# A decoder layer and a linear attention on one core: head rows spread by DMA, one-head blocks written by GpSimd

## The chip, the cores and the metric

The kernel runs on one core of a Trainium2 chip. The metric is the device time of one execution in microseconds. Engines are named as in the profile: PE is TensorE (PEld its weight loads), DVE is VectorE, ACT is ScalarE, POOL is GpSimd, SP is SyncE, which issues most DMAs.

## What is computed

The reference, cut to what matters (names as in the kernel; ln is a layer norm with gain and bias):

```python
def _mha(q_in, k_in, v_in, ..., mask):            # 16 heads of width 8, model width 128
    q = (q_in @ qw + qb).reshape(b, sq, 16, 8).transpose(0, 2, 1, 3)
    k, v = ...                                     # the same from k_in and v_in
    scores = einsum('bhqd,bhkd->bhqk', q, k) / sqrt(8)
    if mask is not None:
        scores = where(mask == 0, -1e9, scores)
    out = einsum('bhqk,bhkd->bhqd', softmax(scores), v)
    return out.transpose(0, 2, 1, 3).reshape(b, sq, 128) @ ow + ob

x = x + mha(x, x, x, mask);        x = ln(x, g1, be1)     # x: 16 x 128 x 128 f32
x = x + mha(x, ctx, ctx, None);    x = ln(x, g2, be2)     # ctx: 16 x 77 x 128
x = x + relu(x @ w1 + b1) @ w2 + b2;  x = ln(x, g3, be3)
# linear attention of x over ctx
KV = elu(ctx).T @ ctx;  Z = 1 / (elu(x) . sum(elu(ctx)) + 1e-6)
out = ln(x + (elu(x) @ KV) * Z, gamma, beta)
```

## The kernel before

The batch of 16 is taken in 8 groups of two items (G = 2). A group goes through a pipeline of iterations: iteration i projects q, k and v of self-attention (kind "s") for group i + 1 (stage NEXT = -1), runs the two self-attention jobs of group i (SELF), the two cross-attention jobs (kind "c") of group i - 1 (CROSS), the feed-forward part and the linear attention of group i - 2 (TAIL) and the output of group i - 3 (LAST). Each iteration has four steps k = 0 to 3, called steps below. In step k one job is "current": s of item 0, s of item 1, c of item 0, c of item 1. For the current job PE forms the scores a second time with keys on the partitions (`key_major`, L344), ACT takes the exponential (L564) and PE multiplies with V (`times_v`, L360). For the job after it PE forms the scores with queries on the partitions (`query_major`, L321) only for the row maxima, which DVE takes (L714). For the job before it PE transposes and projects (L380, L385, L389), DVE adds the residual and takes the moments (L752 to L763), POOL forms the inverse root (`inverse_root`, L942), DVE standardises (L770), and POOL writes the residual of the next stage (`next_residual`, L949, L951). So step 0 prepares maxima for s of item 1, step 1 for c of item 0, step 2 for c of item 1, and step 3 for s of item 0 of the next group.

Each engine has its own queue of instructions, written in the order of the same loops (`iteration` in each engine's block), and stands at the first semaphore wait that is not met. `PROJ_USES` (L86) lists at which step and which quarter u of it a projection or a transpose uses one of two PSUM banks.

A score product contracts over 128 partitions although a head has only 8 columns. Four heads, the "unit" u, are handled together, and q and k are first split into a high and a low bf16 part (`split_hi` on ACT, L597; `split_lo` on DVE, L780). Then the "head rows" are built: for a unit, 32 rows of the four heads are repeated four times over the partitions, as hi/lo of q against hi/lo of k. PE does this by eight products with 0/1 matrices for a kind, side and item (`spread_rows`, L457, products at L465 and L467; the uses sq0, sk0, cq0, ck0 and so on), and ACT copies the result out (`copy_rows`, L600, L611). From the rows of q DVE makes four one-head blocks (`widen`, L785, copies at L790): the rows times a column that is 1 on the partitions of head j and 0 elsewhere (`row_is_j`). `query_major` waits for these blocks (`wide_s`, `wide_c`) of its item and for the rows of k before its first product.

Iterations 3 to 6 are a loop on the device (`run_iterations`, L120), the others are written out.

## Time and profile before

| | us |
|---|---|
| runs (3) | 342.73, 343.69, 345.12; median 343.69 |
| the profiled execution | 342.77 |
| its span in the profile | 340.70 |
| one iteration in the middle | 36.3 |

The profile is of the one execution of 342.77 us; 2.07 us of it lie around the span. The page gives each engine's busy time, and a view of windows gives it for single stretches with the clock granted to TensorE (1.00 is full). The timeline gives instructions in order of time with start and duration; merged ones have a count (x4), and in brackets how long the engine had been idle before and what ended that.

### The profile page before, as it was taken

The numbers are of one execution on the slowest core, as the hardware profiler recorded it, in microseconds if no ns is written. First come the engines' busy times: TensorE is split into PE (matmuls) and PEld (weight loads), VectorE is DVE, ScalarE is ACT, GpSimd is POOL, SyncE is SP. The second block draws the span as 40 slices with busy tenths as digits, with TensorE's granted clock in tenths as the row PEclk, the third lists the DMA queues.
The fourth block names the chain that finished last, engine by engine and source line by source line (L and its number), as shares of the span: only waits on it lengthen the run. The fifth ranks groups of instructions, "written<-read, shape, count | busy, mean of one in ns | idle before, by whom it ended". The sixth has DMA issues, their size and how long they took to land.

```text
span 340.7 us, 8979 instructions
## 1 busy us (share of the span) xinstructions
PE 289.0 (85%) x3056; PEld 197.5 (58%) x3056; DVE 261.5 (77%) x867; ACT 174.5 (51%) x386; POOL 76.0 (22%) x136
## 2 busy tenths in 40 slices
PE   3769789989999999989998999899988986788551
PEld 2534555766775667656665676567755754565331
DVE  7664787878698979898898979897989784765524
ACT  2215445756565566646664656465754655336220
POOL 0410200211132112212231214112222224202421
PEclk9979999999999999999999999999999999589695
DMA  7500000000000000100000000000000000000000
GB/s 223 187 0 3 17 9 3 27 3 9 2 27 3 12 0 17 29 9 0 15 25 9 0 15 25 0 9 0 25 1 11 2 26 2 0 15 11 2 15 15
DMA packets 7506, 6.85 MB, mean 20 GB/s; under 512 B 744, under 2 KB 6712, under 8 KB 7480
## 3 DMA queue, kind: packets, MB, share of 16 engines
q1 hardware_dynamic: 7048, 6.38, 6.3%
q8 instruction: 15, 0.25, 0.3%
q10 hardware_dynamic: 432, 0.14, 0.2%
q14 instruction: 11, 0.09, 0.1%
HBM read 5.46 MB, written 1.05 MB: 19 GB/s over the span
## 4 chain that ended last, share of the span: by engine, by line
PE 54%; DVE 24%; issue 10%; ACT 5%; POOL 3%; DVEq 1%; DMA 1%; ACTq 0%; POOLq 0%; SPq 0%
PE proj_ps L399 10%; PE av_ps L370 7%; DVE neg_max L714 5%; PE s_ps L357 5%; PE s_ps L353 5%; PE s_ps L335 4%; PE proj_ps L465 3%; PE s_ps L332 3%; PE proj_ps L405 3%; POOL rstd L942 3%; PE s_ps L351 3%; PE proj_ps L467 2%; PE post_ps L389 2%; PE proj_ps L424 2%; PE post_ps L385 2%
## 5 line engine op out<-in xcount | busy, mean ns | idle before, releaser
L564 ACT ACTIVATE probs<-s_ps 128x512 f32<-128x512 f32 (+1 forms) x128 | 76.2, 595 | 57.4 <-PE s_ps L357 56.1
L714 DVE TENSOR_REDUCE neg_max<-s_ps 128x4 f32<-128x512 f32 (+1 forms) x128 | 71.6, 576 | 9.5 <-PE s_ps L335 9.2
L942 POOL TENSOR_TENSOR rstd<-var_e,neg_half 128x1 f32<-128x1 f32 x32 | 17.5, 547 | 181.8 <-DVE var_e L763 181.8
L357 PE MATMUL s_ps<-max_x,unit_sel 128*128 128x512 bf16 (+1 forms) x128 | 49.0, 383 | 3.6 <-DVE max_x L728 3.4
L399 PE MATMUL proj_ps<-x_t,w_sb 128*128 128x256 f32 x80 | 26.6, 455 | 1.0 <-issue 0.6
L335 PEld LDWEIGHTS s_ps<-sk_rows,sq_wide 128*128 128x128 bf16 x256 | 20.6, 101 | 10.3 <-issue 1.6
L570 ACT COPY av_sb<-av_ps 128x256 f32<-128x256 f32 x32 | 11.9, 372 | 27.3 <-PE av_ps L370 27.3
L335 PE MATMUL s_ps<-sk_rows,sq_wide 128*128 128x128 bf16 x256 | 25.7, 225 | 0.0
L332 PE MATMUL s_ps<-bias_q,id_b 128*128 128x512 bf16 x64 | 25.4, 397 | 0.0
L353 PE MATMUL s_ps<-cq_wide,ck_rows 128*77 128x512 bf16 x64 | 24.8, 387 | 0.0
L351 PE MATMUL s_ps<-bias_k,id_b 128*128 128x512 bf16 x64 | 24.7, 386 | 0.0
L353 PE MATMUL s_ps<-sq_wide,sk_rows 128*128 128x512 bf16 x64 | 24.5, 383 | 0.0
L728 DVE TENSOR_TENSOR max_x<-s_ps,max_is_j 128x512 bf16<-128x512 bf16 x32 | 22.1, 691 | 2.2 <-PE s_ps L342 2.1
L790 DVE TENSOR_SCALAR sq_wide<-sq_rows,row_is_j 128x512 bf16<-128x512 bf16 x64 | 20.3, 380 | 2.9 <-ACT sq_rows L611 2.9
L370 PE MATMUL av_ps<-probs,v_aug_s 128*32 128x128 f32 x512 | 20.6, 279 | 1.7 <-ACT probs L564 1.7
L357 PEld LDWEIGHTS s_ps<-max_x,unit_sel 128*128 128x128 bf16 (+1 forms) x128 | 13.8, 108 | 14.1 <-DVE max_x L728 7.3
L370 PE MATMUL av_ps<-probs,v_aug_c 77*32 77x128 f32 x512 | 20.6, 279 | 1.4 <-ACT probs L564 1.2
L335 PEld LDWEIGHTS s_ps<-ck_rows,cq_wide 128*128 128x128 bf16 x256 | 17.2, 101 | 6.5 <-DVE neg_max L714 0.3
L619 ACT ACTIVATE hid<-proj_ps,col_sb 128x256 f32<-128x256 f32 x32 | 13.4, 471 | 14.7 <-PE proj_ps L399 14.7
L335 PE MATMUL s_ps<-ck_rows,cq_wide 128*128 128x77 bf16 x256 | 19.9, 203 | 0.2 <-DVE neg_max L714 0.2
L752 DVE TENSOR_TENSOR x_post<-post_ps,r 128x128 f32<-128x128 f32 x32 | 9.2, 288 | 13.4 <-PE post_ps L389 13.3
L399 PEld LDWEIGHTS proj_ps<-x_t,w_sb 128*128 128x128 f32 x80 | 15.4, 217 | 6.0 <-issue 3.4
(131 smaller groups left out, 657.7 us busy)
## 6 DMA issues: line engine op xcount, KB each, us to landing
xt_in<-in_x_t SPq DMA_DIRECT2D x8, 128.0 KB, 2.0
out<-o_all SPq DMA_DIRECT2D x8, 128.0 KB, 1.8
row_sb<-in_rows SPq DMA_DIRECT2D x1, 832.0 KB, 6.5
w_sb<-in_weights SPq DMA_DIRECT2D x1, 768.0 KB, 10.4
ct_in<-in_ctx_t SPq DMA_DIRECT2D x8, 77.0 KB, 1.8
cn_in<-in_ctx_n SPq DMA_DIRECT2D x8, 77.0 KB
w_sb<-in_weights SPq DMA_DIRECT2D x2, 128.0 KB, 2.8
id_f<-in_ident ACTq DMA_DIRECT2D x1, 64.0 KB, 2.6
```

What stands on the lines that cost most here:

```text
L332: nc.tensor.matmul(bank[:, :], id_b[:], bias_q[:].unsqueeze(1).to_broadcast([P, RH, n]), start=True, stop=False, skip_group_check=True)
L335: last = nc.tensor.matmul(bank[:, j * n:(j + 1) * n], wide[kind][:, b, j, u, :], rows_qk[kind + "k"][:, b, u, :], start=(kind == "c"), sto ...
L351: nc.tensor.matmul(bank[:, :], id_b[:], bias_k[:].unsqueeze(1).to_broadcast([P, RH, S]), start=True, stop=False)
L353: nc.tensor.matmul(bank[0:n, :], rows_qk[kind + "k"][:, b, u, :], wide[kind][:, b, :, u, :], start=(kind == "c"), stop=False)
L357: nc.tensor.matmul(bank[0:n, :], unit_sel[:, u, 0:n], max_x[:, b, :, :], start=False, stop=True).then_inc(M["s2_ready"], 1)
L370: last = nc.tensor.matmul(av_ps[32 * r:32 * r + VW, rr * S:(rr + 1) * S], v_aug[kind][:, b, u, r, :], probs[0:KLEN[kind], u, r * S:(r + 1) ...
L399: return nc.tensor.matmul(bank[:, at:at + n], w_sb[:, w, :], src, start=True, stop=True)
L564: nc.scalar.activation(probs[0:n, u, :], s2_ps[u % 2][0:n, :], ACT.Exp, scale=SCALE).then_inc(M["exp_done"], 1)
L714: nc.vector.tensor_reduce(neg_max[:, b, RH * u:RH * (u + 1)], scores, AX_X, ALU.max, negate=True).then_inc(M["max_done"], 1)
L728: nc.vector.tensor_tensor(max_x[:, b, :, :], nmt_ps.unsqueeze(1).to_broadcast([P, RH, S]), max_is_j[:].unsqueeze(2).to_broadcast([P, RH, S ...
L790: last = nc.vector.tensor_scalar(wide[name[0]][:, b, j, :, :], rows_qk[key][:, b, :, :], row_is_j[:, j:j + 1], None, ALU.mult)
L942: nc.gpsimd.tensor_tensor(rstd[:, b, :], var_e[:, b, :], neg_half[:, 0:1], ALU.pow).then_inc(M["rstd_ready"], 1)
```

## The change

Three things change together. First, the head rows are no longer spread by PE. The columns of the q and k weights and biases are permuted on the host, so that the row of head j, column c, unit u lies at partition (j, c, u) with u innermost, and four DMAs from SBUF to SBUF for each side write the rows: repeat s goes to partitions s, s + 4, s + 8 and so on. That is eight DMAs for each kind and group, all issued by SP. The products with 0/1 matrices, their two PSUM uses and ACT's copies go. Second, the one-head blocks are written by POOL, for both items of a group at once: four instructions of 1024 elements (4 units x 2 items x 128) for each kind and group. Kind c is written in step 0, after `next_residual` of that step; kind s in steps 1 and 2, two heads each, after `next_residual`. Third, what that needs: blocks and k rows have two buffers (group parity), so have `xt_in` and `ct_in`, which are loaded an iteration earlier, and all twelve iterations are written out, with no loop.

```diff
-        ("yc0", TAIL, 0, 0), ("cv", CROSS, 0, 0), ("cq0", CROSS, 0, 1), ("ck0", CROSS, 0, 2), ("sqk", NEXT, 0, 3),
...
+        ("yc0", TAIL, 0, 0), ("cv", CROSS, 0, 0), ("sqk", NEXT, 0, 3),
...
-    def run_iterations(eng, iteration):
-
-        for i in range(NEXT, TAIL + 1):
-            iteration(i)
-        with eng.Fori(TAIL + 1, NG - 1) as i:
-            iteration(i)
-        for i in range(NG - 1, NG + LAST):
+    def run_iterations(iteration):
+
+        for i in range(NEXT, NG + LAST):
             iteration(i)
...
-                rows_qk[key] = sb(f"{key}_rows", [P, G, UNITS, n], BF16)
-            wide[kind] = sb(f"{kind}q_wide", [P, G, RH, UNITS, S], BF16)
+            rows_k[kind] = sb(f"{kind}k_rows", [P, 2, UNITS, G, KLEN[kind]], BF16)
+            rows_q[kind] = sb(f"{kind}q_rows", [P, UNITS, G, S], BF16)
+            wide[kind] = sb(f"{kind}q_wide", [P, 2, RH, UNITS, G, S], BF16)
...
+        def wait_spread(eng, key, g):
+
+            eng.wait_ge(M["spread_" + key], 16 * 4 * (g + 1))
...
+            def spread_rows(i, name):
+
+                kind = name[0]
+                g = i - (NEXT if kind == "s" else SELF)
+                wait_read(sp, i, name)
+                wait_reuse(sp, M["wide_" + kind], RH * g)
+                for s in range(4):
+                    sp.dma_start(rows_q[kind][s:P:4, :, :, :].rearrange("p u b n -> p u (b n)"),
+                                 part_of(kind + "q", s)[:].rearrange("p b n -> p (b n)")).then_inc(
+                        M[f"spread_{kind}q"], 16)
+                s2_done(sp, kind, g - 2)
+                for s in range(4):
+                    sp.dma_start(rows_k[kind][s:P:4, g % 2, :, :, :].rearrange("p u b n -> p u (b n)"),
+                                 part_of(kind + "k", s)[:].rearrange("p b n -> p (b n)")).then_inc(
+                        M[f"spread_{kind}k"], 16)
...
                 if u == 0:
-                    pe.wait_ge(M[f"wide_{kind}"], G * g + b + 1)
-                    wait_rows(pe, kind, "k", b, g)
+                    pe.wait_ge(M["wide_" + kind], RH * (g + 1))
+                    wait_spread(pe, kind + "k", g)
...
-                for u in range(UNITS):
-                    nc.tensor.matmul(bank[:, u * n:(u + 1) * n], spread[side, "hi"][:, u, :, :],
-                                     hi[kind + side][:, b, :], start=True, stop=False)
...
-                nc.scalar.copy(rows_qk[name[:2]][:, b, :, :], proj_ps[bank_of(name)][:, 0:UNITS * n].rearrange(
-                    "p (u n) -> p u n", u=UNITS)).then_inc(read(name), 1)
...
-                for j in range(RH):
-                    last = nc.vector.tensor_scalar(wide[name[0]][:, b, j, :, :], rows_qk[key][:, b, :, :],
-                                                   row_is_j[:, j:j + 1], None, ALU.mult)
...
+            def widen(kind, g, heads):
+
+                wait_spread(pool, kind + "q", g)
+                s2_done(pool, kind, g - 2)
+                for j in heads:
+                    nc.gpsimd.tensor_scalar(wide[kind][:, g % 2, j, :, :, :], rows_q[kind][:], row_is_j[:, j:j + 1],
+                                            None, ALU.mult).then_inc(M["wide_" + kind], 1)
...
                     if prev:
                         inverse_root(*prev)
                         next_residual(*prev)
+                    if k == 0 and on(i, CROSS):
+                        widen("c", i - CROSS, range(RH))
+                    if k in (1, 2) and on(i, NEXT):
+                        widen("s", i - NEXT, range(2 * k - 2, 2 * k))
...
+    rows_first = np.arange(d).reshape(UNITS, RH, hd).transpose(1, 2, 0).reshape(d)
+    for n in ("sa_qw", "sa_kw", "ca_qw", "ca_kw", "sa_qb", "sa_kb", "ca_qb", "ca_kb"):
+        a[n] = a[n][..., rows_first]
```

How the order moves, first on POOL, from step 0 to step 2 of an iteration in which all stages run. Before (rstd, y_g and r are the inverse root, the product with the gain and the residual; rstd_l and rstd_f belong to the last two norms):

```order
L942 TENSOR_TENSOR rstd<-var_e,neg_half 128x1
L949 TENSOR_TENSOR y_g<-y_n,row_sb 128x128
L951 TENSOR_TENSOR r<-y_g,res_bias 128x128
L960 TENSOR_TENSOR rstd_l<-var_l,neg_half 128x2
L942 TENSOR_TENSOR rstd<-var_e,neg_half 128x1
L949 TENSOR_TENSOR y_g<-y_n,row_sb 128x128
L951 TENSOR_TENSOR r<-y_g,res_bias 128x128
L964 TENSOR_TENSOR rstd_f<-var_f,neg_half 128x2
L942 TENSOR_TENSOR rstd<-var_e,neg_half 128x1
```

And now, at the same place:

```order
L934 TENSOR_TENSOR r<-y_g,res_bias 128x128
L920 TENSOR_SCALAR cq_wide<-cq_rows,row_is_j 128x1024 x4
L945 TENSOR_TENSOR rstd_l<-var_l,neg_half 128x2
L925 TENSOR_TENSOR rstd<-var_e,neg_half 128x1
L932 TENSOR_TENSOR y_g<-y_n,row_sb 128x128
L934 TENSOR_TENSOR r<-y_g,res_bias 128x128
L920 TENSOR_SCALAR sq_wide<-sq_rows,row_is_j 128x1024 x2
L949 TENSOR_TENSOR rstd_f<-var_f,neg_half 128x2
L925 TENSOR_TENSOR rstd<-var_e,neg_half 128x1
L932 TENSOR_TENSOR y_g<-y_n,row_sb 128x128
L934 TENSOR_TENSOR r<-y_g,res_bias 128x128
L920 TENSOR_SCALAR sq_wide<-sq_rows,row_is_j 128x1024 x2
```

The four copies of kind c stand behind the residual of step 0, the four of kind s behind those of steps 1 and 2.

On PE, the end of step 0 and the first products of step 1, with their waits. Before (nm_parts are the maxima being transposed, the two products with xt_in are the projection sqk, and L335 is the first product of `query_major` for kind c):

```order
L342 MATMUL s_ps<-id_b,nm_parts 128x128 [waits nm_ready]
L485 ISA
L118 REGISTER_ALU [waits xt_loaded]
L399 MATMUL proj_ps<-xt_in,w_sb 128x256 [waits proj_read0]
L399 MATMUL proj_ps<-xt_in,w_sb 128x256
L325 ISA
L252 REGISTER_ALU [waits wide_c]
L118 ISA [waits proj_read1]
L335 MATMUL s_ps<-ck_rows,cq_wide 128x77 [waits max_done]
```

And now:

```order
L365 MATMUL s_ps<-id_b,nm_parts 128x128 [waits nm_ready]
L422 MATMUL proj_ps<-xt_in,w_sb 128x256 [waits proj_read0,xt_loaded0]
L422 MATMUL proj_ps<-xt_in,w_sb 128x256
L358 MATMUL s_ps<-ck_rows,cq_wide 128x77 [waits max_done,spread_ck,wide_c]
L358 MATMUL s_ps<-ck_rows,cq_wide 128x77 x3
L393 MATMUL av_ps<-probs,v_aug_s 32x128 [waits exp_done]
```

The place of the first product of step 1 on PE is the same; its wait now asks for the blocks of both items, written by POOL, and for the k rows from the DMAs.

## Rows read from the trace of the kernel before

**Rows 1.** Page, part 1: engine busy us (share of the span) xinstructions.

```profile
PE 289.0 (85%) x3056; PEld 197.5 (58%) x3056; DVE 261.5 (77%) x867; ACT 174.5 (51%) x386; POOL 76.0 (22%) x136
```

**Rows 2.** Windows: length, busy PE, PEld, DVE, ACT, POOL (xcount), granted clock.

```profile
21.00:24.20 3.20, 3.20 (x15) 1.71 (x14) 1.68 (x3) 0.60 (x1) 0.00 (x0) 0.50 0.00 0
163.34:199.67 36.33, 34.37 (x384) 23.73 (x383) 31.43 (x106) 21.45 (x48) 8.69 (x17) 1.00 0.04 12
```

**Rows 3.** Groups by line and shape, VectorE: the copies into one-head blocks.

```profile
L790 DVE TENSOR_SCALAR sq_wide<-sq_rows,row_is_j 128x512 bf16<-128x512 bf16 x64 | 20.3, 380 | 2.9 <-ACT sq_rows L611 2.9
L790 DVE TENSOR_SCALAR cq_wide<-cq_rows,row_is_j 128x512 bf16<-128x512 bf16 x64 | 18.2, 347 | 0.4 <-ACT cq_rows L611 0.3
```

**Rows 4.** Timeline (start us, us, engine, line), steady iteration, spread by TensorE.

```profile
173.99 0.22 PE L465 MATMUL proj_ps<-sq_hi,spread_q_hi 128*128 128x128 bf16 x1
174.44 0.39 PE L380 MATMUL post_ps<-id_f,av_sb 128*128 128x128 f32 x2
...
187.94 0.21 PE L465 MATMUL proj_ps<-ck_hi,spread_k_hi 128*128 128x77 bf16 x1
188.23 0.46 PE L389 MATMUL post_ps<-w_sb,att_t 128*128 128x128 f32 x2
```

**Rows 5.** Timeline, steady iteration, step 0 into step 1.

```profile
190.15 0.55 POOL L942 TENSOR_TENSOR rstd<-var_e,neg_half 128x1 f32<-128x1 f32 x1 [6.25 <-DVE var_e L763]
190.15 0.30 PE L335 MATMUL s_ps<-ck_rows,cq_wide 128*128 128x77 bf16 x4
...
191.83 0.45 POOL L951 TENSOR_TENSOR r<-y_g,res_bias 128x128 f32 x1 [0.22 <-POOL y_g L949]
```

**Rows 6.** Timeline, same iteration, step 2 into step 3.

```profile
171.87 0.38 PE L332 MATMUL s_ps<-bias_q,id_b 128*128 128x512 bf16 x1
...
172.25 0.55 POOL L942 TENSOR_TENSOR rstd<-var_e,neg_half 128x1 f32<-128x1 f32 x1 [3.52 <-DVE var_e L763]
...
173.91 0.45 POOL L951 TENSOR_TENSOR r<-y_g,res_bias 128x128 f32 x1 [0.19 <-POOL y_g L949]
```

**Rows 7.** Groups by line and shape, GpSimd, and the tile sq_rows (min/median/max ns).

```profile
L949 POOL TENSOR_TENSOR y_g<-y_n,row_sb 128x128 f32<-128x128 f32 x32 | 14.8, 461 | 14.8 <-DVE y_n L770 14.8
...
L934 POOL TENSOR_TENSOR r<-x_all,row_sb 128x2048 f32<-128x2048 f32 x1 | 4.5, 4507 | 11.9 <-DMA x_all<-in_x 11.9
...
L790 DVE TENSOR_SCALAR sq_wide<-sq_rows,row_is_j x64: 341/346/2100, 9.6 to 250.0; 128x512 bf16<-128x512 bf16 x64
```

**Rows 8.** Timeline, start of the program.

```profile
11.57 0.63 PE L332 MATMUL s_ps<-bias_q,id_b 128*128 128x512 bf16 x1
...
15.33 3.28 DVE L790 TENSOR_SCALAR sq_wide<-sq_rows,row_is_j 128x512 bf16<-128x512 bf16 x4
...
17.71 0.49 POOL L936 TENSOR_TENSOR res_bias<-row_sb 128x128 f32<-128x128 f32 x1
...
19.69 0.23 PE L342 MATMUL s_ps<-id_b,nm_parts 128*128 128x128 bf16 x1 [4.12 <-DVE nm_parts L721]
...
20.34 0.38 PE L351 MATMUL s_ps<-bias_k,id_b 128*128 128x512 bf16 x1
```

**Rows 9.** Timeline, iteration 0 and iteration 8.

```profile
39.98 0.46 POOL L951 TENSOR_TENSOR r<-y_g,res_bias 128x128 f32<-128x128 f32 x1
...
43.95 0.10 PEld L342 LDWEIGHTS s_ps<-id_b,nm_parts 128*128 128x128 bf16 x1 [1.45 <-DVE nm_parts L721]
...
292.36 0.68 PE L335 MATMUL s_ps<-ck_rows,cq_wide 128*128 128x77 bf16 x8
...
295.13 0.45 POOL L951 TENSOR_TENSOR r<-y_g,res_bias 128x128 f32<-128x128 f32 x1
```

**Rows 10.** Page, part 6 (KB each, us to landing), and timeline: DMA issue and low parts.

```profile
xt_in<-in_x_t SPq DMA_DIRECT2D x8, 128.0 KB, 2.0
...
12.23 0.43 SPq L304 DMA_DIRECT2D ct_in<-in_ctx_t  x1
...
180.34 0.37 DVE L780 SCALAR_TENSOR_TENSOR ck_lo<-proj_ps,col_sb,ck_hi 128x154 bf16<-128x154 f32 x1
```

More of the change, by code:

```diff
@@ L86, in decoder_layer_kernel @@
     PROJ_USES = [
-        ("yc0", TAIL, 0, 0), ("cv", CROSS, 0, 0), ("cq0", CROSS, 0, 1), ("ck0", CROSS, 0, 2), ("sqk", NEXT, 0, 3),
-        ("yc1", TAIL, 1, 0), ("cq1", CROSS, 1, 0), ("ck1", CROSS, 1, 1), ("h01", TAIL, 1, 1), ("h23", TAIL, 1, 2),
-        ("ff", TAIL, 1, 4),
-        ("ys0", SELF, 2, 0), ("sq0", NEXT, 2, 0), ("sk0", NEXT, 2, 1), ("kv", TAIL, 2, 2), ("sv", NEXT, 2, 3),
-        ("yt", TAIL, 2, 4),
-        ("ys1", SELF, 3, 0), ("sq1", NEXT, 3, 0), ("sk1", NEXT, 3, 1), ("cqk", SELF, 3, 2), ("la", TAIL, 3, 3)]
+        ("yc0", TAIL, 0, 0), ("cv", CROSS, 0, 0), ("sqk", NEXT, 0, 3),
+        ("yc1", TAIL, 1, 0), ("h01", TAIL, 1, 1), ("h23", TAIL, 1, 2), ("ff", TAIL, 1, 4),
+        ("ys0", SELF, 2, 0), ("kv", TAIL, 2, 2), ("sv", NEXT, 2, 3), ("yt", TAIL, 2, 4),
+        ("ys1", SELF, 3, 0), ("cqk", SELF, 3, 2), ("la", TAIL, 3, 3)]
     USE_NAMES = [name for name, *_ in PROJ_USES]
@@ L144, in decoder_layer_kernel @@
         id_b = sb("id_b", [P, P], BF16)
-        spread = {(side, part): sb(f"spread_{side}_{part}", [P, UNITS, 4, 32], BF16)
-                  for side in "qk" for part in ("hi", "lo")}
         row_is_j = sb("row_is_j", [P, RH])
@@ L541, in iteration @@
                     light_work(i, k, UNITS)
-            run_iterations(pe, iteration)
+            run_iterations(iteration)
         @block.scalar
@@ L676, in _ @@
                 nc.vector.memset(v_aug[kind][:], 0.0)
-            for tile in spread.values():
-                nc.vector.memset(tile[:], 0.0)
             nc.vector.memset(cn_in[:, :, D:D + 1], 1.0).then_inc(M["zeros_set"], 1)
```

115 lines of the change are left out of this document (48 added, 67 removed).

## The prediction

> **What bounds the kernel now.** I read the page's busy shares first, then the windows of single iterations, then the timeline of one steady iteration line by line, and last the start and the end. The page shows TensorE (PE) at 85% and VectorE (DVE) at 77%, ScalarE (ACT) at 51%, and GpSimd (POOL) at 22% [rows 1]. In a steady iteration, from 163.34 to 199.67, it is clearer: of 36.33 us PE is busy 34.37 and DVE 31.43, at the full clock, and POOL only 8.69 [rows 2]. So PE's queue sets the pace: 1.96 us of it are idle. By that view it looks right to take work from PE and DVE and give some to POOL. The timeline must say whether POOL gives it back in time, since PE takes its instructions in order and stands at the first wait that is not met.
>
> **What is removed.** PE's spread of head rows goes: eight matmuls of 128 columns take from 173.99 to 174.44, 0.45 us, and eight of 77 columns from 187.94 to 188.23, 0.29 us [rows 4]. A steady iteration has six of the first kind (sq0, sq1, sk0, sk1, cq0, cq1) and two of the second (ck0, ck1): 6 x 0.45 + 2 x 0.29 = 3.3 us of PE. ACT's eight copies out of PSUM behind them go, and DVE's sixteen copies into one-head blocks, 20.3 + 18.2 us in all [rows 3], which is 4.8 us for each of 8 groups. PE's 1.96 us of idle time come mostly from waits on such ACT and DVE work; I take 1.5 us of them as gained. Together 4.8 us for each of the iterations 2 to 6, that is 24 us. Iterations 0, 1, 7 and 8 hold only parts of this work; I put them at 8 us together (1, 2.5, 2.5, 2). Gain: 32 us.
>
> **What is added on the DMA queue.** Sixteen DMAs for a group. A neighbouring row shows 0.43 us to issue one, and 2.0 us for 128 KB to land [rows 10]; each new one moves 64 KB (or 39) in 128 pieces. Four q DMAs are thus in place about 4 x 0.43 + 2.0 = 3.7 us after the low part is written, all eight after 5.4. For kind c the low part ends at 180.71 [rows 10] and POOL first turns to the rows at 192.28 [rows 5]: 11.6 us of cover. For kind s the cover is about step 0's end to step 1's end, nearly as much. The DMAs cost nothing unless each takes some 3 us by itself. The second buffer of xt_in and ct_in, and the unrolled loop, I put at nothing: PE hardly waits for loads, and iterations written out in the program before (2, and 7 on) look like the loop's.
>
> **What is added on POOL, and where.** Each group and kind now has four POOL instructions of 1024 elements. No row shows this operation on POOL. With two f32 inputs it takes 461 ns for 128 elements and 4507 ns for 2048 [rows 7], so (4507 - 461) / 1920 = 2.11 ns an element and 191 ns fixed; 1024 elements would be 2.35 us, the upper end. The lower end is DVE's own pace for it: 18.2 us for 64 copies of 512 elements [rows 3], 0.284 us each, so 0.57 us for 1024. The new instruction reads one stream, not two; half the slope gives 0.191 + 1024 x 1.055 ns = 1.27 us. I take T = 1.27, as the row of the same engine is nearer than DVE's.
>
> What matters is the place in the queue. At step 0 POOL does rstd, y_g and the residual r for the job before, and then the four copies of kind c, with no wait between. DVE's and POOL's part of that chain begins with PE's L389 of the same step and can't come earlier: L389 starts at 188.23 [rows 4], rstd at 190.15, y_g follows, r ends at 191.83 + 0.45 = 192.28 [rows 5]. But PE comes to the first product that needs the c blocks (L335, the first of step 1) at 190.15 [rows 5]. The blocks are there at 192.28 + 4T. PE therefore stands still for 2.13 + 4T = 7.2 us. In the kernel before, DVE writes these blocks during step 0, and only those of one batch item.
>
> At step 2 the same happens with kind s. Half of its copies come at step 1, where they are harmless (rstd_f comes about when they end). The other two come after r of step 2, which ends at 173.91 + 0.45 = 174.36, while PE is at step 3's first product (L332) at 171.87 [rows 6]: 2.49 + 2T = 5.0 us of waiting. Behind both waits stand PE's remaining key-major products and products with V, for which ACT and DVE wait in turn, so nothing makes these 12.2 us good; PE's work before and after is full.
>
> Ends without the pattern: **start.** POOL is held by r0 and the two bias sums until 17.71 + 0.49 = 18.20 [rows 8]; then come 4T, so the first product starts at 23.3 where it was 11.57. The way from there to the first L351 was 8.8 us; without DVE's 3.28 us of widening and PE's spread about 4.8. So L351 comes at 28.1 where it was 20.34: 7.8 us. **Iteration 0:** r ends at 40.44, blocks at 43.0, four products with their maxima then take about 4.4 us to L342, against 43.95 [rows 9]: 3.4 us. **Iteration 1:** c has no residual ahead, but its DMAs and 4T take about 9 us: 3 us; s as above, 5.0. **Iterations 2 to 6:** 5 x 12.2 = 61.2. **Iteration 7:** c, 7.2. **Iteration 8:** r ends at 295.58, PE is there at 292.36 [rows 9]: 3.2 + 4T = 8.3. Sum of waits: 95.9 us.
>
> **The clock.** At the start PE stood for 4.12 us before 19.69 [rows 8], and the stretch from 21.00 to 24.20 then ran at 0.50 of the clock, 1.2 GHz where it was 2.4 before, with PE busy all the time [rows 2]. Such a stretch costs 3.1 / 2 = 1.55 us. Twelve to fourteen of the new waits are longer than that one: 13 x 1.55 = 20 us.
>
> Sum, against the profiled execution's 342.77 us: - 32 + 95.9 + 20 = 427. The runs' median is 343.69; I forecast **427 us**, 24% slower.
>
> **Where the skill is weighed.** The rows put one POOL copy between 0.57 and 2.35 us. The Trainium skill, "GPSIMD Engine Reference", Performance versus the Vector engine, gives a port-bound 1.03 cycles an element for a short one-input body and 769 ns measured for 512 elements; by the first figure an estimate of T is 1.07 us and the sum 417, by the second twice 769 ns, 1.54 us, and 440. No run here shows either. In [rows 8] four DVE copies took 3.28 us instead of 4 x 0.284 = 1.14 beside a long POOL instruction, one of them 2100 ns [rows 7]; "SBUF — State Buffer" calls this pair of ports an exclusive lock, and the trace agrees. It can delay single DVE instructions by up to T here, at times when DVE has slack, so it changes neither sum nor chances.
>
> **Rivals.** The sum has 50 us for each us of T (4 at the start, 2 + 4 + 2 in iterations 0 and 1, 30 in 2 to 6, 4 + 4 at the end).
> (a) *POOL needs the two-input time*, T = 2.35: 427 + 54 = 481. For it: it is the engine's only measured slope. Against: half the data is read, in bf16.
> (b) *Shorter copies and no clock loss*: at T = 0.57 the waits are 4.4 and 3.6 us; 427 - 35 - 20 = 372. For it: such short waits are near or below the one that cost the clock. T = 1.27 with no clock loss gives 407.
> (c) *The DMAs are late*: if each of the q DMAs of kind c took 4 us one after another, 16 us against 11.6 of cover, 4.4 us more for 7 groups: 458. Against: issue and landing in [rows 10].
> (d) *Not slower: the blocks are ready when PE comes*, so that only the gain is left, 343 - 32 = 311 us. The place is PE's first product of steps 1 and 3. It decides where 2.13 + 4T and 2.49 + 2T fall to nothing; no T does that, since r alone ends after PE arrives. It needs PE to reach these products later than now for another reason, above all that it is held by DVE's maxima. Without clock loss the sum breaks even at T of about 0.1 us, less than any POOL row.
>
> **How the numbers follow.** Forecast (T from 0.9 to 1.6, with most of the clock loss: 405 to 445) 0.62; (a), T well above that, 0.13; (b), 372 to 405, 0.17; (c) 0.04; (d) 0.03, and 0.01 that the parts cancel. The range, 388 to 470, leaves out the outer half of (a) and of (b). About 1% is what a measurement can tell here: faster 0.03, same 0.01, slower 0.96.
>
> **What would show it.** Right: PE idle before L358 (the old L335 and, with its bias, L332) and put down to POOL's widening or its row copies, 7 and 5 us long, once each an iteration; POOL's four copies back to back at 1.27 us each right behind r; an iteration of some 47 us; a granted clock of 0.5 in parts; PE, DVE and ACT busy for smaller shares. Wrong: copies of POOL that end before PE arrives, waits on the DMAs in their place, iterations near 31 us.

## The result and the profile after

The changed kernel takes 533.64 us (median of 4 runs, 532.5 to 535.74) against 344.02 us of the kernel before on the same chip: ratio 1.552, 95% interval 1.544 to 1.560. The forecast was 427 us with a range of 388 to 470. The sign and the place were right, the size was not. The profiled execution took 532.5 us, with a span of 530.7.

The page of the kernel after, part 1 and the granted clock of part 2, against [rows 1]:

```profile
PE 295.0 (56%) x2522; PEld 190.6 (36%) x2544; DVE 233.4 (44%) x727; ACT 145.6 (27%) x322; POOL 257.0 (48%) x200
...
PEclk9998586878696959578687959578686958955876
```

PE has 534 matmuls fewer and is yet busy for longer, since part of them ran at half the clock (the run e6 below has the same 2522 recorded matmuls in 260.5 us). POOL's 76.0 us have become 257.0. No engine is busy for much more than half of the span, which says that they wait for each other in turn. The chain of the work that ended last says for whom:

```profile
POOL 37%; PE 36%; DVE 15%; issue 7%; DMA 2%; ACT 1%; SPq 1%; POOLq 0%; DVEq 0%
POOL cq_wide L920 17%; POOL sq_wide L920 13%; PE av_ps L393 6%; PE proj_ps L422 5%; PE s_ps L358 5%; PE s_ps L376 4%; PE s_ps L355 3%; POOL rstd L925 3%; PE s_ps L380 3%; PE s_ps L374 2%; DMA x_all<-in_x 2%; DVE y_n L757 2%; DVE st L745 2%; PE post_ps L412 2%; DVE x_post L739 2%
```

The groups of POOL's copies (L920; busy and mean of one, then idle time before) and PE's waits (total, times, longest):

```profile
L920 POOL TENSOR_SCALAR cq_wide<-cq_rows,row_is_j 128x1024 bf16<-128x1024 bf16 x32 | 90.5, 2849 | 10.9 <-DMA cq_rows<-cq_lo 10.9
L920 POOL TENSOR_SCALAR sq_wide<-sq_rows,row_is_j 128x1024 bf16<-128x1024 bf16 x32 | 90.9, 2853 | 0.1
```

```profile
PE s_ps L358 <- POOL cq_wide L920: 101.8, 8, 14.6
PE s_ps L355 <- POOL sq_wide L920: 78.9, 8, 22.9
```

One copy takes 2.85 us. I had taken 1.27 and set 2.35 as the upper end. PE waits for them 8 + 8 times, 180.7 us together, where I had summed 95.9 (at the start the 22.9 us are the whole wait, while my sum counts only the delay). In the timeline of a middle iteration the places are those of [rows 5] and [rows 6]: r, then the copies in one piece, then PE.

```profile
245.44 0.45 POOL L934 TENSOR_TENSOR r<-y_g,res_bias 128x128 f32<-128x128 f32 x1
245.87 11.31 POOL L920 TENSOR_SCALAR cq_wide<-cq_rows,row_is_j 128x1024 bf16<-128x1024 bf16 x4
257.24 0.44 PE L358 MATMUL s_ps<-ck_rows,cq_wide 128*128 128x77 bf16 x4 [12.93 <-POOL cq_wide L920]
...
279.08 0.45 POOL L934 TENSOR_TENSOR r<-y_g,res_bias 128x128 f32<-128x128 f32 x1
279.51 5.67 POOL L920 TENSOR_SCALAR sq_wide<-sq_rows,row_is_j 128x1024 bf16<-128x1024 bf16 x2
285.24 0.61 PE L355 MATMUL s_ps<-bias_q,id_b 128*128 128x512 bf16 x1 [6.55 <-POOL sq_wide L920]
```

That iteration (243.90 to 303.23) lasts 59.33 us where 36.33 were before [rows 2]. The windows show it whole, then the first wait, and the three stretches behind idle time at about half the clock (the last columns are granted clock, DMA share, GB/s):

```profile
243.90:303.23 59.33, 35.77 (x316) 23.20 (x319) 29.01 (x90) 17.92 (x41) 31.35 (x25) 0.80 0.09 24
...
247.00:257.20 10.20, 0.00 (x0) 0.00 (x0) 0.00 (x0) 0.00 (x0) 10.18 (x4) 0.55 0.18 51
```

```profile
257.20:262.00 4.80, 4.76 (x37) 2.81 (x38) 1.95 (x9) 1.73 (x4) 0.00 (x0) 0.53 0.00 0
...
275.50:278.70 3.20, 3.18 (x14) 2.24 (x12) 2.72 (x10) 0.97 (x2) 0.70 (x2) 0.50 0.02 5
285.20:289.30 4.10, 4.06 (x31) 2.39 (x32) 0.81 (x2) 0.97 (x2) 1.39 (x2) 0.53 0.00 0
```

From 247.0 to 257.2 not one instruction runs on PE, DVE or ACT. The half clock covers 12.1 us of the iteration, PE nearly always busy in them, so by an estimate it adds some 6 us.

### The profile page after: what moved, and what is told of

Read it like the earlier page. It is cut to its first block, busy times and chain, and to the rows that moved or that the text cites. A ratio compares the mean times of both kernels' runs of the same rounds, so it can differ in the third digit from the quotient of the medians.

```text
span 530.7 us, 7271 instructions
## 1 busy us (share of the span) xinstructions
PE 295.0 (56%) x2522; PEld 190.6 (36%) x2544; DVE 233.4 (44%) x727; ACT 145.6 (27%) x322; POOL 257.0 (48%) x200
## 3 DMA queue, kind: packets, MB, share of 16 engines
HBM read 5.46 MB, written 1.05 MB: 12 GB/s over the span
## 4 chain that ended last, share of the span: by engine, by line
POOL 37%; PE 36%; DVE 15%; issue 7%; DMA 2%; ACT 1%; SPq 1%; POOLq 0%; DVEq 0%
POOL cq_wide L920 17%; POOL sq_wide L920 13%; PE av_ps L393 6%; PE proj_ps L422 5%; PE s_ps L358 5%; PE s_ps L376 4%; PE s_ps L355 3%; POOL rstd L925 3%; PE s_ps L380 3%; PE s_ps L374 2%; DMA x_all<-in_x 2%; DVE y_n L757 2%; DVE st L745 2%; PE post_ps L412 2%; DVE x_post L739 2%
## 5 line engine op out<-in xcount | busy, mean ns | idle before, releaser
L920 POOL TENSOR_SCALAR cq_wide<-cq_rows,row_is_j 128x1024 bf16<-128x1024 bf16 x32 | 90.5, 2849 | 10.9 <-DMA cq_rows<-cq_lo 10.9
L920 POOL TENSOR_SCALAR sq_wide<-sq_rows,row_is_j 128x1024 bf16<-128x1024 bf16 x32 | 90.9, 2853 | 0.1
L358 PE MATMUL s_ps<-ck_rows,cq_wide 128*128 128x77 bf16 x256 | 22.9, 223 | 105.1 <-POOL cq_wide L920 101.8
L355 PE MATMUL s_ps<-bias_q,id_b 128*128 128x512 bf16 x64 | 30.2, 472 | 85.1 <-POOL sq_wide L920 78.9
L358 PEld LDWEIGHTS s_ps<-ck_rows,cq_wide 128*128 128x128 bf16 x256 | 19.1, 115 | 116.7 <-POOL cq_wide L920 104.8
L380 PE MATMUL s_ps<-max_x,unit_sel 128*77 128x512 bf16 (+1 forms) x106 | 45.0, 424 | 0.0
L355 PEld LDWEIGHTS s_ps<-bias_q,id_b 128*128 128x128 bf16 x64 | 7.2, 113 | 84.0 <-POOL sq_wide L920 58.2
L358 PE MATMUL s_ps<-sk_rows,sq_wide 128*128 128x128 bf16 x256 | 30.0, 250 | 0.0
L358 PEld LDWEIGHTS s_ps<-sk_rows,sq_wide 128*128 128x128 bf16 x256 | 24.1, 115 | 14.4 <-issue 8.6
L374 PE MATMUL s_ps<-bias_k,id_b 128*128 128x512 bf16 x64 | 26.9, 420 | 0.0
L393 PE MATMUL av_ps<-probs,v_aug_c 77*32 77x128 f32 x512 | 24.1, 314 | 1.4 <-ACT probs L570 1.2
L932 POOL TENSOR_TENSOR y_g<-y_n,row_sb 128x128 f32<-128x128 f32 x32 | 14.8, 463 | 15.0 <-DVE y_n L757 15.0
L945 POOL TENSOR_TENSOR rstd_l<-var_l,neg_half 128x2 f32<-128x2 f32 x8 | 6.4, 804 | 31.9 <-DVE var_l L801 31.9
```

The lines of the kernel that those rows point to most:

```text
L355: nc.tensor.matmul(bank[:, :], id_b[:], bias_q[:].unsqueeze(1).to_broadcast([P, RH, n]), start=True, stop=False, skip_group_check=True)
L358: last = nc.tensor.matmul(bank[:, j * n:(j + 1) * n], wide[kind][:, g % 2, j, u, b, :], rows_k[kind][:, g % 2, u, b, :], start=(kind == "c ...
L374: nc.tensor.matmul(bank[:, :], id_b[:], bias_k[:].unsqueeze(1).to_broadcast([P, RH, S]), start=True, stop=False)
L380: nc.tensor.matmul(bank[0:n, :], unit_sel[:, u, 0:n], max_x[:, b, :, :], start=False, stop=True).then_inc(M["s2_ready"], 1)
L393: last = nc.tensor.matmul(av_ps[32 * r:32 * r + VW, rr * S:(rr + 1) * S], v_aug[kind][:, b, u, r, :], probs[0:KLEN[kind], u, r * S:(r + 1) ...
L920: nc.gpsimd.tensor_scalar(wide[kind][:, g % 2, j, :, :, :], rows_q[kind][:], row_is_j[:, j:j + 1], None, ALU.mult).then_inc(M["wide_" + ki ...
```

## The experiments

Theory: the time is PE's waits for POOL's copies right behind r, so it follows their place and their price T. Rivals: the row DMAs or their issue; the clock; the written-out loop; VectorE held by POOL; and that the gain I had assumed is not there. "Middle iteration" is one of the iterations 2 to 6. The kernel before, measured beside these runs, had medians of 343.4 to 344.7 us. e2 to e5 and e11 were executed once each, the others four times or more. e2 and e6 leave out scores, so they are no kernels to be used, only measurements.

**e1, one part undone: VectorE widens.**

```diff
-                    if k == 0 and on(i, CROSS):                 # POOL
-                        widen("c", i - CROSS, range(RH))
-                    if k in (1, 2) and on(i, NEXT):
-                        widen("s", i - NEXT, range(2 * k - 2, 2 * k))
+                if k == 0 and u in (2, 3) and on(i, CROSS):     # VectorE
+                    widen("c", i - CROSS, range(2 * u - 4, 2 * u - 2))
+                if k == 2 and u < 4 and on(i, NEXT):
+                    widen("s", i - NEXT, [u])
```

> The changed kernel with one thing undone: the one-head blocks are written by VectorE again (four instructions of 1024 elements for a kind and group: kind c at quarters 2 and 3 of step 0, kind s one in each quarter of step 2). The DMAs, the double buffers and the written-out iterations stay. Theory (all of the loss is PE's wait for POOL's copies, and what the clock loses behind it; spreading by DMA is the gain I worked out): the waits for widening are under 1 us each, PE's 3.3 us of spreading an iteration are gone, and VectorE, busy 31.4 us of a 36.3-us iteration before, sets the pace: iterations of 32 to 34 us, total 322 us (312 to 335). Rival A (the sixteen DMAs of a group or SP's 0.6 us for each are part of the loss): PE or VectorE waits on the row DMAs, over 360 us. Rival B (the written-out loop costs): over 345 with no waits of this kind.

Measured: 359.46 us, ratio 1.045 (1.039 to 1.051). POOL's part is 174 of the 190 us, as the theory says. But nothing of a gain is to be seen behind it: without POOL's copies the kernel is still 15 us slower than before. The theory's 322 missed. Rival A does not hold either: a middle iteration has no wait on row DMAs. The time fits rival B's, but not its cause, as e14 shows. PE does 3.4 us less and the iteration takes 37.31 us:

```profile
200.03:237.34 37.31, 30.96 (x320) 20.29 (x318) 30.45 (x98) 17.82 (x40) 9.12 (x16) 1.00 0.13 36
```

PE waited 1.8 and 1.4 us for blocks that VectorE writes last in their step, and 1.7 us for `att`.

**e2, half of the dose.** Heads 1 and 3 of each unit are left out of the widening.

```diff
-                        widen("c", i - CROSS, range(RH))
+                        widen("c", i - CROSS, range(0, RH, 2))
...
-                        widen("s", i - NEXT, range(2 * k - 2, 2 * k))
+                        widen("s", i - NEXT, [2 * k - 2])
```

> The changed kernel with POOL writing the blocks of heads 0 and 2 of each unit only; the blocks of heads 1 and 3 stay zero, so half of the scores are left out of the widening, with PE's products unchanged. It halves the number of POOL copies at every place. Theory (the time follows 4T, 2T and the like, with T = 2.85 us measured, 50 T in the sum): half of 50 x 2.85 = 71 us less, 462 us (450 to 475); PE's wait at L358 7.2 us and at L355 3.7 us in a middle iteration, where they are 12.9 and 6.6. Rival (the waits are set by something else that POOL's widening only happens to follow, or another wait takes the place): 500 us or more.

Measured: 448.76 us, 85 us less, and waits in a middle iteration of 7.3 and 3.7 us. The waits came out as expected. The time is just below the expected 450 to 475: it fell by more than the 50 T of the sum.

**e3, PE kept busy in the waits.**

```diff
+                    if b == 0 and (kind == "c" or g > 0):
+                        for _ in range(46 if kind == "c" else 22):
+                            nc.tensor.matmul(s1_ps[0][:, :], id_b[:], bias_q[:].unsqueeze(1).to_broadcast([P, RH, S]),
+                                             start=True, stop=True, skip_group_check=True)
                     pe.wait_ge(M["wide_" + kind], RH * (g + 1))
```

> The changed kernel with PE doing idle products of 512 columns into the free score bank ahead of the two waits for the blocks, 46 of them (9.9 us at 0.216 us each) before L358 of kind c, 22 (4.75 us) before L355 of kind s. Waits end when POOL ends, as before, but PE is not idle in them. Theory (of the 534 us some 40 are products at half the clock behind the waits): in a middle iteration of the changed kernel the stretches 257.2 to 261.9 and 285.2 to 289.2 run at half clock, which is 2.3 + 2.0 us; gone, they give 4.3 us for each of 7 iterations, total 503 us (495 to 512). Rival (the half clock is beside the path, the pace is set by POOL and VectorE): 530 or more.

Measured: 524.62 us, 9 us less, and middle iterations of 58.0 to 58.2. The expectation of 503 missed. The filling ended 3 us before the blocks came, and the clock fell behind it all the same, only later and for less time (two windows of that run):

```profile
197.80:200.40 2.60, 2.56 (x31) 1.77 (x32) 0.94 (x3) 0.97 (x2) 0.00 (x0) 0.77 0.00 0
200.40:203.00 2.60, 2.60 (x12) 1.82 (x11) 1.86 (x10) 1.36 (x3) 0.72 (x1) 0.57 0.03 6
```

So this run took away only part of what it was to take away. It shows that the clock is a share of the loss, not its size. The size is read better from e6, which has the same 316 recorded products in a middle iteration: PE is busy for 30.36 us there, and for 35.77 in the iteration shown above, 5.4 us more.

**e4, the price of a copy by itself.**

```diff
+            then(nc.gpsimd.tensor_scalar(tb[1][:, 0:1024], tb[0][:, 0:1024], c0, None, ALU.mult))
+            then(nc.gpsimd.tensor_scalar(tb[1][:, 0:512], tb[0][:, 0:512], c0, None, ALU.mult))
...
```

> The changed kernel, and behind its last store eleven instructions on POOL alone, nothing else running, each behind the one before, to price the copy: with a column as the factor 1024, 512 and 2048 bf16 elements; with a constant as the factor, 1024 bf16; with a column, 1024 f32; a plain copy of 1024 bf16 and of 1024 f32; the product of two tensors of 1024, f32 and bf16. Theory (the price is POOL's own, by element, and neither VectorE nor the DMAs lengthen it): the 1024-element one takes 2.85 us as inside the kernel, 512 take 1.5, 2048 take 5.6; f32 in place of bf16 about the same or less; the f32 product of two tensors 2.35 us by the slope read before (rows of r0 and of y_g). Rival (it is long only in the kernel, by contention for SBUF): 1.3 us or less for 1024 alone.

The timeline of POOL, behind the last store, with nothing else running (0/1 column as the factor for 1024, 512 and 2048; a constant; f32; plain copies; products of two tensors):

```profile
535.67 2.85 POOL L979 TENSOR_SCALAR tb<-tb,row_is_j 128x1024 bf16<-128x1024 bf16 x1
538.62 1.56 POOL L980 TENSOR_SCALAR tb<-tb,row_is_j 128x512 bf16<-128x512 bf16 x1
540.28 5.44 POOL L981 TENSOR_SCALAR tb<-tb,row_is_j 128x2048 bf16<-128x2048 bf16 x1
545.80 2.77 POOL L982 TENSOR_SCALAR tb<-tb 128x1024 bf16<-128x1024 bf16 x1
548.67 2.84 POOL L983 TENSOR_SCALAR tf<-tf,row_is_j 128x1024 f32<-128x1024 f32 x1
551.58 1.04 POOL L984 COPY tb<-tb 128x1024 bf16<-128x1024 bf16 x1
552.67 1.04 POOL L985 COPY tf<-tf 128x1024 f32<-128x1024 f32 x1
553.80 2.34 POOL L986 TENSOR_TENSOR tf<-tf 128x1024 f32<-128x1024 f32 x1
556.22 2.12 POOL L987 TENSOR_TENSOR tb<-tb 128x1024 bf16<-128x1024 bf16 x1
```

Alone it takes the same 2.85 us: no contention. From 512 to 2048 elements it grows by 3.88 / 1536 = 2.53 ns an element, with 0.27 us fixed. The type makes no difference to it, a constant factor almost none. With one stream it is dearer than the product of two tensors (2.34), whose slope I had halved. A plain copy costs 1.04.

**e5, the lower price in the same places.** Since a head's rows lie on 32 partitions of their own, plain copies of these into blocks zeroed once give the same blocks.

```diff
-                    nc.gpsimd.tensor_scalar(wide[kind][:, g % 2, j, :, :, :], rows_q[kind][:], row_is_j[:, j:j + 1],
-                                            None, ALU.mult).then_inc(M["wide_" + kind], 1)
+                    nc.gpsimd.tensor_copy(wide[kind][32 * j:32 * j + 32, g % 2, j, :, :, :],
+                                          rows_q[kind][32 * j:32 * j + 32]).then_inc(M["wide_" + kind], 1)
...
```

> The changed kernel with POOL's product with a 0/1 column replaced by a plain copy of the 32 partitions of the head into blocks that are zeroed once at the start; same places, same number (four for kind c behind r in step 0, two and two for kind s in steps 1 and 2). A plain copy of 1024 bf16 elements took 1.04 us alone, so T goes from 2.85 to 1.04, below the 1.27 us that I had assumed. Theory (place right, T wrong): by the slope of the run with half of the heads, (533.6 - 448.8) / 1.43 = 59 us for each us of T, 533.6 - 1.81 x 59 = 426 us; by the prediction's own sum 427 - 0.23 x 50 = 415. So 410 to 432, with waits of 5.7 us at L358 and 3.0 us at L355 in a middle iteration. Rival (a fixed cost of the POOL path, not the price of its copies): over 460.

Measured: 435.43 us, just above the expected 410 to 432, with waits of 6.0 and 4.2 us in a middle iteration. From here to the changed kernel it is 98.2 us for 1.81 us of T, 54 for each; the prediction's sum had 50.

**e6, no widening at all** (the scores are left out; VectorE zeroes the blocks once at the start, and PE waits for the row DMAs).

```diff
-                    pe.wait_ge(M["wide_" + kind], RH * (g + 1))
+                    wait_spread(pe, kind + "q", g)
...
+            for kind in "sc":
+                nc.vector.memset(wide[kind][:], 0.0)
...
```

> The changed kernel with the widening left out altogether: the blocks stay zero, PE waits for the row DMAs of q and k alone. So all products, maxima and DMAs remain and the scores are left out. It shows what spreading by DMA can give at most, my 'gain of 32 us'. By the prediction 343.5 - 32 = 311 us, somewhat less still, as VectorE's 4.5 us of widening an iteration are gone too. Rival, after the run with VectorE's widening came at 359 with PE idle 6.4 us of a 37.3-us iteration: PE's freed time turns into waits for the round trips through VectorE and ScalarE and for the DMAs, so 325 to 340. Rival C: the start alone (rows by DMA are later than by PE) costs some 4 us of either.

Measured: 334.85 us, ratio 0.970 (0.966 to 0.975). So without any widening the gain is 9 us, not 32; the forecast's 311 missed, and the rival's 325 to 340 holds. A middle iteration, and PE's only long wait for blocks or rows, at the start:

```profile
153.32:187.12 33.80, 30.36 (x316) 20.37 (x319) 27.16 (x90) 17.71 (x41) 8.72 (x17) 1.00 0.15 42
```

```profile
PE s_ps L354 <- DMA sk_rows<-sk_lo: 18.0, 1, 18.0
```

But this start is not that of the changed kernel: e6's own zeroing delays it. Its timeline, and then the first row DMA of the changed kernel:

```profile
3.88 3.47 DVE L671 MEMSET sq_wide<- 128x4096 uint32 x1 [0.80 <-issue]
8.15 3.47 DVE L671 MEMSET cq_wide<- 128x4096 uint32 x1 [0.80 <-issue]
13.01 4.52 DVE L691 TENSOR_SCALAR bias_q<-mask_q_i 128x128 bf16<-128x128 int32 x1
17.45 0.47 DVE L768 SCALAR_TENSOR_TENSOR sq_lo<-proj_ps,col_sb,sq_hi 128x256 bf16<-128x256 f32 x1
18.34 1.27 SPq L277 DMA_DIRECT2D sq_rows<-sq_hi  x2
```

```profile
10.09 1.27 SPq L278 DMA_DIRECT2D sq_rows<-sq_hi  x2
```

The row DMAs start 8.25 us later than in the changed kernel. An estimate without this delay is 334.9 - 8.2 = some 327 us, a ceiling of 17 us for the gain; it was not run.

**e7, the two kinds divided** (plain copies; kind s on POOL, all four in step 1; kind c on VectorE at quarters 1 and 2 of step 0) and **e8, all on VectorE** (plain copies, kind s at quarters 0 and 1 of step 2).

```diff
+                if k == 0 and u in (1, 2) and on(i, CROSS):     # VectorE, both runs
+                    widen("c", i - CROSS, range(2 * u - 2, 2 * u))
+                    if k == 1 and on(i, NEXT):                  # POOL, e7
+                        widen("s", i - NEXT, range(RH))
+                if k == 2 and u in (0, 1) and on(i, NEXT):      # VectorE, e8
+                    widen("s", i - NEXT, range(2 * u, 2 * u + 2))
```

> The plain copies of 32 partitions, divided: kind s by POOL, all four behind r in step 1 (4 x 1.04 = 4.2 us, wanted only at step 3), kind c by VectorE at quarters 1 and 2 of step 0, earlier than in the run in which VectorE did all. Nothing of POOL's copies stands between r and a product that waits. Theory: PE's waits for blocks under 1 us each, iterations of 34 us instead of 37.3, total 335 us (325 to 345). Rival (VectorE and ScalarE round trips set the pace whatever the blocks do): 350 or more. It is also the candidate for a kernel that beats the one before.

> Both kinds by VectorE with the plain copies of 32 partitions, kind c at quarters 1 and 2 of step 0, kind s at quarters 0 and 1 of step 2, two at a time. Against the first run (VectorE, product with a column, 525 ns each, later places, 359.5 us) it changes place and price. If a plain copy takes about half, 0.27 us, VectorE has 2 us more in an iteration: 338 us (328 to 348). Rival (place and price don't matter, the round trips do): 352 to 360.

Measured: 355.81 us (ratio 1.034, 1.029 to 1.038) and 360.26 us (1.043, 1.037 to 1.049). Both missed. Earlier and cheaper copies bring a middle iteration at the full clock down to 35.4 us in e7 and 35.7 in e8, below the 36.33 before. But the start is 11 us later than before (the first rstd begins at 43.99 and 44.55, in the kernel before at 33.31), and not all middle iterations ran at the full clock: one of e7's five took 38.6 us and three of e8's 38.7, each at a granted clock of 0.91. e8's trace is of the slowest of its four executions, 363.12 us.

**e9, other places at the lower price.**

```diff
+                    if k == 0 and on(i, CROSS):
+                        widen("c", i - CROSS, range(RH))
                     if prev:
                         inverse_root(*prev)
                         next_residual(*prev)
-                    if k == 0 and on(i, CROSS):
-                        widen("c", i - CROSS, range(RH))
-                    if k in (1, 2) and on(i, NEXT):
-                        widen("s", i - NEXT, range(2 * k - 2, 2 * k))
+                    if k == 1 and on(i, NEXT):
+                        widen("s", i - NEXT, range(RH))
```

> The run with POOL's plain copies (435.4 us, T = 1.04) with only POOL's order changed: kind c's four copies stand ahead of the inverse root of step 0, in the time in which POOL waited for var_e, and kind s's four all behind r of step 1. Price and number of the copies stay. Theory (at either price the loss is in the place: right behind r, and r ends after PE is there): c's rows land some 4 us before the inverse root's turn, so 4 x 1.04 us nearly fit, PE's waits at L358 and L355 are under 1 us in a middle iteration, iterations of 34 to 35 us against 33.8 with no widening at all, total 340 us (334 to 349). Rival (POOL's copies slow the others wherever they stand, by the port or by delaying POOL's own chain): 355 or more.

Measured: 360.50 us (1.053, 1.046 to 1.060). 75 us of e5's loss go with the place. But the expected 340 missed, and the rival's 355 or more holds: e9 stays 26 us above e6. Three of the five middle iterations take 35.3 to 35.5 us, and this is what POOL does from its new place, by the timeline of POOL and VectorE:

```profile
166.35 4.31 POOL L921 COPY cq_wide<-cq_rows 32x1024 bf16<-32x1024 bf16 x4 [0.90 <-POOL r L936]
...
166.90 0.68 DVE L701 TENSOR_REDUCE neg_max<-s_ps 128x4 f32<-128x512 f32 x1
...
168.63 0.96 DVE L706 CAST nm_parts<-neg_max 128x16 bf16<-128x16 f32 x1
169.62 1.05 DVE L708 TENSOR_TENSOR nm_parts<-neg_max,nm_parts 128x16 bf16<-128x16 f32 x1
```

The last two VectorE instructions take 0.17 us each elsewhere. Beside POOL's copies each lasts as long as one of them, and the maxima that PE waits for come 1.7 us later. That is the difference between such an iteration and e6's 33.8, and no more. In the two profiled executions e9 ends 20.8 us behind e6: it is 11 us behind where the middle iterations begin, loses some 1.6 us in three of them, and 5.9 in the one that took 39.7 us at a granted clock of 0.91.

**e10, an earlier start** (the first low parts ahead of VectorE's memsets, the first blocks on VectorE).

```diff
+            split_lo(NEXT, "sqk", "s")
             nc.vector.memset(nm_parts[:], 0.0)
```

> The run before this one in the list, and the start rearranged: VectorE writes the low parts of the first q and k ahead of its memsets (they were at 17.4 us, behind a VectorE instruction held for 4.5 us beside POOL's first residual), and the first four blocks of kind s are written by VectorE, not behind POOL's first residual. Theory: the first product with blocks comes at about 18 to 20 us instead of 25 to 26, so 5 to 7 us less: 334 us (328 to 342), 2 to 4% below the kernel before. Rival (the row DMAs at the start queue behind the weights and x, so nothing is won): no change against the run before it.

Measured: 356.80 us (1.036, 1.030 to 1.042), 3.7 us less than e9; the expected 334 missed. Its premise was wrong: low parts at 17.4 us are e6's. In e9 the first row DMA is issued at 10.65 us, in e10 at 10.24. And the first blocks came later, not earlier, so that PE's first product with them starts at 26.30 us, in e9 at 23.12: the plain copy that takes VectorE 417 ns elsewhere (e8, kind c) took 2443 beside POOL's long instructions (first residual, then a memset). Where the 3.7 us come from is not shown.

```profile
L814 DVE COPY sq_wide<-sq_rows 32x1024 bf16<-32x1024 bf16 x4 | 9.8, 2443 | 4.7 <-issue 4.6
```

**e11, the other places at the full price**, the changed kernel with e9's order.

> The changed kernel with only POOL's order changed in the same way (kind c ahead of the inverse root of step 0, kind s all four behind r of step 1), with the product by a column at T = 2.85. It fills the square of place and price. Theory: 4 x 2.85 = 11.4 us of copies for c begin when the rows land, some 4 us before PE wants them: a wait of about 7 us in place of 12.9, for s about 3.5 in place of 6.6, but now the inverse root and r stand behind the c copies. Iterations of 48 to 51 us, total 455 us (435 to 480), against 533.6. Rival (POOL's sum of work, 31.4 us an iteration, makes the place worthless): over 500.

Measured: 470.82 us. The square of place and price, in us (middle iteration in brackets):

| | T = 2.85 | T = 1.04 |
|---|---|---|
| right behind r | 533.6 (59.3 to 60.5) | 435.4 (47.2 to 48.0) |
| ahead of the inverse root, and step 1 | 470.8 (49.5 to 51.0) | 360.5 (34.6 to 35.5, one 39.7) |

with 334.9 (33.8) for no copies. At T = 1.04 POOL also zeroes the blocks once, 6.9 us for each kind. Place and price both count, and the place is worth 63 to 75 us at either price.

**e12, blocks by DMA**: 16 DMAs of 32 source partitions for the q rows straight into the blocks, and **e13, with the earlier start**.

```diff
-                    sp.dma_start(rows_q[kind][s:P:4, :, :, :].rearrange("p u b n -> p u (b n)"),
+                    for j in range(RH):
+                        sp.dma_start(wide[kind][32 * j + s:32 * j + 32:4, g % 2, j, :, :, :].rearrange(
+                            "p u b n -> p u (b n)"), part_of(kind + "q", s)[32 * j:32 * j + 32].rearrange(
...
```

> The changed kernel with no widening by any engine: the q rows go by DMA straight into the one-head blocks (zeroed once at the start), 16 DMAs of 32 source partitions for a kind and group in place of 4, all issued by SP, k rows as before. Theory: with no engine copying, iterations come to those of the run without widening, 33.8 us, and the total to 335 us (332 to 345), provided that SP issues a quarter-sized DMA in a third of a microsecond or less (0.62 us for the 64-KB ones). Rival (issue cost is fixed at 0.6 us for each DMA): 16 x 0.6 + 4 x 0.6 + 2 = 14 us from the low part to the last row, c's rows come some 5 us late, iterations of 39 us or more, total over 365.

> The run before this one in the list, with the first low parts written by VectorE ahead of its memsets, so that the first row DMAs are issued at about 10 us and not at 18. VectorE no longer waits there beside POOL's first residual. Theory: the first block product moves from about 28 us to 20, the total falls by 6 to 8 us to 328 (322 to 338), 4% below the kernel before. Rival (queued behind the weights, or the next chain of the start takes over): less than 2 us of difference.

Measured: 416.76 us (1.210, 1.207 to 1.213) and 417.04 us. The rival was right, and more than right: a DMA of 16 KB costs SP more than one of 64 KB (0.60 us). The timeline of SP's queue (duration for eight, and for one DMA of k rows, 38.5 KB), with PE's wait for kind c:

```profile
186.42 6.11 SPq L280 DMA_DIRECT2D cq_wide<-cq_hi  x8
192.59 5.69 SPq L280 DMA_DIRECT2D cq_wide<-cq_lo  x8
198.33 0.58 SPq L284 DMA_DIRECT2D ck_rows<-ck_hi  x1
...
202.21 0.42 PE L359 MATMUL s_ps<-ck_rows,cq_wide 128*128 128x77 bf16 x4 [7.07 <-issue]
```

Middle iterations of e12 take 41.5 to 42.6 us. That e13 changes nothing was to be expected by the traces: e12's first small DMA was issued at 10.48 us already, e13's at 10.46.

**e14, the kernel before, written out.**

```diff
-        with eng.Fori(TAIL + 1, NG - 1) as i:
-            iteration(i)
-        for i in range(NG - 1, NG + LAST):
+        for i in range(NEXT, NG + LAST):
             iteration(i)
```

> The kernel before with its loop of iterations 3 to 6 written out, nothing else changed. I had put this at nothing. Theory: within 1% of the kernel before, 340 to 347 us. Rival (written-out code costs fetches, part of the missing gain): 348 or more, with PE waiting on issue.

Measured: 342.12 us, ratio 0.995 (0.993 to 0.997). The loop was rightly put at nothing.

**e15, each writer where it has slack** (kind s by small DMAs from group 1 on, kind c and the first blocks of kind s by VectorE), and **e16, the small DMAs from group 3 on.** The main line that e16 changes in e15:

```diff
-                if kind == "s" and g > 0:
+                if kind == "s" and g > 2:
```

> Blocks of kind s by DMA straight from the low and high parts (16 small DMAs, 12 us of issue at the 0.73 us measured for each, against 18 us from the low part to the first product that wants them), blocks of kind c by VectorE with plain copies at quarters 1 and 2 of step 0 (4 x 0.42 us), the first blocks of kind s also by VectorE, the first low parts early; POOL widens nothing. Theory: no instruction of POOL holds VectorE any more, and no wait for blocks in a middle iteration, so 34.3 to 35 us each; first product at about 20 us; total 338 us (331 to 346). Rival (VectorE's 1.7 us of copies at the turn of the step shift its maxima, as in the run that divided the kinds): iterations of 35.5 us, total 350.

> The run before it, but blocks of kind s of the groups 0 to 2 by VectorE from rows spread by 4 DMAs, only groups 3 to 7 by the 16 small ones. Theory (what was lost against the kernel before lay in iterations 0 and 1 at SP): 15 us less than 357, 342 us (338 to 347), thus the kernel before within its noise or 1% below. Rival (the middle and the end lose too): 350 or more.

Measured: 357.07 us (1.038, 1.033 to 1.042) and 346.21 us (1.006, 1.003 to 1.009). e15's middle iterations are 34.8 to 35.5 us; it lost in iterations 0 and 1, as e16 shows by giving 11 of the 13 us back. The best kernel with rows by DMA is thus just behind the kernel before: no version here that computes all scores beats it by more than the 0.5% of e14.

## Why the prediction was right and wrong

**The place and the sign: right.** PE stands before L358 in step 1 and L355 in step 3, once each in an iteration, put down to POOL's widening. The square shows the place as a cause: the same copies cost 63 to 75 us less elsewhere.

**The step that failed: the price of a copy.** "The new instruction reads one stream, not two; half the slope gives" 1.27 us, and 2.35 as the upper end. Measured: 2.85 in the kernel and alone (e4). Neither one stream in place of two nor bf16 made it cheap; what counts is the operation (2.84 us for the product with a column, 2.34 for that of two tensors, 1.04 for a plain copy, all f32). My upper end was no bound, since it was another operation's price, and I had argued only downward from it. By the measured 54 us for each us of T the 1.58 us missing are 85 of the 107 us between 427 and 534. By the same slope T = 1.27 would have given about 435.4 + 0.23 x 54 = 448, an estimate, inside the range.

**The gain: a second step that failed.** I put it at 32 us; e6 shows 9, and some 17 by the estimate without e6's own delay. In a middle iteration I had 3.3 us of PE's work and "1.5 us of" its idle time. PE's busy time did fall, by 34.37 - 30.36 = 4.0 us, but its idle time rose from 1.96 to 3.44 us: what PE no longer computes it waits for, at `att`, the maxima and the denominators of VectorE. That leaves 2.5 us instead of 4.8, five times, so some 11 of the missing 15 us. The rest lies outside the middle iterations and was not taken apart. At the start the traces show that rows by DMA come later than rows by PE: e1, without e6's zeroing, has its first rstd at 37.73 us, the kernel before at 33.31.

**The waits, given T: their sum was right, in part by luck.** 95.9 + 50 x 1.58 = 175 us. The 180.7 us measured count the whole first wait of 22.9, where my sum has the delay of the start. That delay is 14.9 us (first L374 at 35.19, L351 before at 20.34), against 7.8 + 4 x 1.58 = 14.1, so the sum to compare is 172.7. Within it errors cancel. The five middle iterations have 99.4 where 108.6 was due: 2.13 + 4T and 2.49 + 2T would be 13.5 and 8.2, and measured are 12.9 and mostly 6.6 to 6.7, since PE, slower in between, comes a little later. Iteration 0 has 11.2 where 6.6 was due.

**The clock: mechanism right, size too small.** I had 1.55 us for each of 13 waits, 20 us in all and 3.1 in a middle iteration. The windows give about 6 there, three stretches of 3.2 to 4.8 us, one of them (275.5 to 278.7) not behind one of my two waits. e6 confirms it: for the same 2522 recorded matmuls PE is busy for 295.0 us in the changed kernel and for 260.5 in e6, 34.5 us more. e3 won back no more than 2 us an iteration, as it removed only part. A middle iteration closes with them: 33.8 (e6) + 12.9 + 6.6 + 6 = 59.3. Over the whole run, 334.9 + (180.7 - 18.0 that e6 waits at the start too) leaves 36 of 533.6 for the clock and all else, close to the 34.5.

**The DMAs: right for these, for a reason that has a limit.** The 64-KB DMAs took 0.60 us to issue, not the 0.43 of [rows 10], and landed in 1.9; only once, in iteration 1, did POOL wait for them (10.9 us). But e12 shows the cover gone as soon as there are 16.

**Rivals.** (a), T at the two-input time, had 481; by its own condition the truth lay beyond it. (b) and (d) fall with T and with [rows 5]; e6 is what (d) would have been, 335 (or some 327), not 311. The break-even that I named for (d) was added up wrongly: -32 + 95.9 - 50 x (1.27 - T) is zero at T = 0, not 0.1, which changes nothing in the argument. (c) fell. The loop cost nothing (e14).

**The port, left out of the sum.** I had said that POOL's hold "changes neither sum nor chances". In the changed kernel that was nearly so, since VectorE mostly stood anyway: 29.0 us busy against e6's 27.2. It was wrong as a general remark: once the waits were gone, this hold was part of what kept e9 and e10 from e6's time, 1.7 us in a middle iteration of e9.

## What to carry to other kernels

Before work is moved to a less busy engine, price the very operation there, alone, with its operands and shape; a neighbour's price is neither an upper nor a lower bound. Then ask when the work may begin and who waits for its end: here the same copies cost 75 us more behind the residual than ahead of the inverse root. And test the gain by leaving the moved work out altogether, since of 4.0 us freed on the busiest engine only 2.5 may be left when others follow close behind. Then compare that test's start with the kernel's own: here what it added, the zeroing, hid some 8 us of the gain.
